# Ten per-head scalings of a delta-rule front moved from VectorE to ScalarE, head by head

## The reference

```
x  = hidden + attention(layernorm(hidden));  out = x + experts(layernorm(x))

# attention, per head h
q, k, v = silu(conv(xn @ W)) each;  q, k = q/|q|, k/|k|;  beta = sigmoid(xn @ Wb)
for each token t:
    u = beta * (v - k . S);   S = S + k u^T;   o = q . S
out = (o normalized per head) @ Wo
```

## Time and profile before

| what | value |
|---|---|
| median of 3 executions | 1375.21 us (1373.84 to 1380.05) |
| the profiled execution | 1386.45 us, its span 1384.7 us |
| mean granted TensorE clock over the span | 0.968 of full speed |
| share of the span busy | PE 96%, DVE 63%, ACT 27%, POOL 24% |
| PE, DVE, ACT busy in 200 to 250 us | 47.41, 37.13, 25.32 of 50 us |
| PE, DVE, ACT busy in 300 to 350 us | 45.91, 43.10, 25.93 of 50 us |

### The profile page before, as it was taken

The page is one execution under the profiler, slowest core; times in us unless marked ns, Lnnn a source line. Parts: engine busy times, 40 slices in busy tenths (PEclk is TensorE's granted clock), DMA queues, the critical chain, the costliest instruction groups (busy, mean ns, idle before and its releaser), DMA issues.

```text
span 1384.7 us, 27271 instructions
## 1 busy us (share of the span) xinstructions
PE 1329.5 (96%) x8490; PEld 841.0 (61%) x8491; DVE 867.6 (63%) x2418; ACT 371.2 (27%) x794; POOL 338.6 (24%) x396
## 2 busy tenths in 40 slices
PE   8979999999999999999999999999999999999996
PEld 7857777887777556544444455555555555555553
DVE  4896687559556512725311177777777777777774
ACT  4635554545443223212000011111111111111111
POOL 1201223223121221311565112221222122222222
PEclk9989999999998799999999999999999999999998
DMA  4205643734474794397545746656766665664430
GB/s 154 61 6 112 100 91 77 133 93 95 89 122 114 137 236 107 70 164 244 189 179 206 244 78 129 136 128 132 176 149 134 126 133 128 131 133 76 70 52 5
DMA packets 208513, 171.05 MB, mean 124 GB/s; under 512 B 71472, under 2 KB 160560, under 8 KB 208432
## 3 DMA queue, kind: packets, MB, share of 16 engines
q1 hardware_dynamic: 135056, 114.16, 33.7%
q0 software_dynamic: 16496, 34.23, 12.7%
q10 hardware_dynamic: 56880, 21.54, 7.7%
HBM read 91.06 MB, written 82.73 MB: 126 GB/s over the span
## 4 chain that ended last, share of the span: by engine, by line
PE 52%; DVE 2%; issue 0%; POOLq 0%; DVEq 0%; ACT 0%
PE pD L2059 15%; PE pG L2039 13%; PE pU L2048 13%; PE pG L2003 3%; PE pU L2003 3%; PE pD L2022 3%; DVE ups L1950 1%; PE pU L1997 0%; PE pD L2017 0%; POOLq L1777 0%; DVE w L1676 0%; DVE w L1677 0%; DVE route_keep L1675 0%; DVE q L1695 0%; DVE qf L1688 0%
## 5 line engine op out<-in xcount | busy, mean ns | idle before, releaser
L1950 DVE STREAM_TRANSPOSE ups<-a 32x96 f32<-32x96 f32 (+1 forms) x1264 | 330.1, 261 | 42.9
L1847 POOL DMA_INDIRECT out<-y,ix x79 | 123.0, 1556 | 481.3 <-ACT y L1903 332.7
L2059 PE MATMUL pD<-w,ups 128*128 (+1 forms) x474 | 218.3, 596 | 3.6 <-DVE ups L1950 3.6
L2039 PE MATMUL pG<-w,xsT 128*128 x632 | 199.9, 458 | 0.0
L2048 PE MATMUL pU<-w,xsT 128*128 x632 | 199.9, 459 | 0.0
L2039 PEld LDWEIGHTS pG<-w,xsT 128*128 128x128 f32 x632 | 119.5, 189 | 88.4 <-issue 37.6
L902 PE MATMUL pProj<-front_region 128*128 128x256 f32 x624 | 159.5, 400 | 2.2 <-ACT front_region L682 1.4
L2048 PEld LDWEIGHTS pU<-w,xsT 128*128 128x128 f32 x632 | 120.1, 190 | 66.9
L2059 PEld LDWEIGHTS pD<-w,ups 128*128 128x128 f32 (+1 forms) x474 | 90.7, 192 | 97.8 <-issue 81.5
L1243 DVE SCALAR_TENSOR_TENSOR front_region<-front_region,cw 128x256 f32<-128x256 f32 x288 | 132.4, 501 | 15.5 <-ACT front_region L698 12.1
L902 PEld LDWEIGHTS pProj<-front_region 128*128 128x128 f32 x624 | 115.8, 195 | 21.8 <-ACT front_region L698 2.9
(11 more groups left out here) (236 smaller groups left out, 1623.2 us busy)
## 6 DMA issues: line engine op xcount, KB each, us to landing
w<-in_up_T SPq DMA_DIRECT2D x16, 1408.0 KB, 6.7
slot_rows<-zeros SPq DMA_DIRECT2D x79, 266.0 KB
xs<-slot_rows ACTq DMA_DIRECT2D x316, 64.0 KB
w<-in_down_T SPq DMA_DIRECT2D x16, 512.0 KB, 8.7
front_region<-in_L_attn_hidden_states SPq DMA_DIRECT2D x16, 256.0 KB, 3.1
x2r<-in_L_attn_hidden_states SPq DMA_DIRECT2D x16, 256.0 KB, 5.5
partial_sums<-x2r SPq DMA_DIRECT2D x16, 256.0 KB, 3.6
x_normed<-x2n SPq DMA_DIRECT2D x16, 256.0 KB, 2.6
```

What stands on the lines that cost most here:

```text
L1847: pool.indirect_dma_start(out=flat, out_offset=bass.IndirectOffsetOnAxis(ap=ix[1 - par][:, 0:1], axis=0), in_=y[1 - par][:, :], in_offset= ...
L1950: dve.transpose(aT[par][B * to:B * to + B, 0:n, rows], a[rows, 0:len(IC) * P].rearrange("p (c n) -> p c n", c=len(IC))[:, 0:n, B * to:B * ...
L2039: mm = pe.matmul(pG[0][:, 0:I], xsT[par][:, k, :], w[:, bass.ds(slot, 1), 2 * I * k:2 * I * k + I], start=(k == 0), stop=(k == DC - 1))
L2059: mm = pe.matmul(pYq[:, :], aT[1 - par][0:m, c, :], down[0:m, :, UPW + D * c:UPW + D * (c + 1)], start=(c == 0), stop=(c == 2))
```

## The change

Six tiles' values (6, 7, 10, 11, 14, 15) and four tiles' Gram blocks (8, 9, 12, 13) are scaled on ScalarE. There a factor is one number for each partition, so that each head is an instruction of its own: eight `activation` of 128x64 with a factor from `sqk` or `ng` in place of one `tensor_tensor` of 128x512 on VectorE. They stand in these places: values of the even tile in slot 5 of the even unit (2, 6, 10), behind `raw_copy`; values of the odd tile in slot 0 of the odd unit (3, 7, 11), behind `x_copy`; Gram blocks in slots 3 and 5 of units 3 and 7, behind `oT_copy` in slot 3 and ahead of `w_copy` in slot 5. The semaphores and what waits for them are as before.

```diff
--- before.py
+++ after.py
@@ -60,6 +60,7 @@
 NUP = DC + 2 * DC * (UNITS - 1)
 NMM = NUP + TPG * UNITS
 EARLY_MM = NMM + DC + 2 * DC
+V_ON_ACT, GRAM_ON_ACT = (6, 7, 10, 11, 14, 15), (8, 9, 12, 13)
 FILL_AT, FILL = (11, 3), 2
 XG_AT = SHARED_W
 SA_AT = XG_AT + 2 * DC * GN
@@ -681,6 +682,26 @@
                 least(act, s_bp, p - 1)
                 act.activation(xnT[p % 2][:, :, tok(t)], quads(pT0[:, 0, :]), ACT.Copy).then_inc(s_xnT, 1)
 
+            def scale_v(t):
+                act.wait_ge(s_vtp, t + 1)
+                act.wait_ge(s_coef, t // 2 + 1)
+                least(act, s_R, 2 * (t - VH_RING) + 2)
+                for h in range(H):
+                    ins = act.activation(vh[t % VH_RING][:, cols(h)], pT0[:, 0, cols(h)], ACT.Copy,
+                                         scale=sqk[t // 2 % 2][:, H * (t % 2) + h:H * (t % 2) + h + 1])
+                ins.then_inc(s_vh, 1)
+
+            def scale_blocks(t):
+                act.wait_ge(s_G, t + 1)
+                act.wait_ge(s_ng, t // 2 + 1)
+                least(act, s_Xp, t - NP_RING + 1)
+                for f in range(2):
+                    for n in range(HH):
+                        h = H * (t % 2) + 2 * n + f
+                        ins = act.activation(NP[t % NP_RING][:, cols(HH * f + n)], pG[:, f, cols(n)], ACT.Copy,
+                                             scale=ng[t // 2 % 4][:, h:h + 1])
+                ins.then_inc(s_N, 1)
+
             def tanh(p):
                 act.wait_ge(s_bp, p + 1)
                 least(act, s_hb, p)
@@ -814,6 +835,10 @@
                         x_copy(u)
                     if even and s == (0 if pk else 1) and pair_ok(pk) and pk != 1:
                         tanh(pk)
+                    if even and s == 5 and 2 * old in V_ON_ACT and old > 1:
+                        scale_v(2 * old)
+                    if not even and s == 0 and u + 4 in V_ON_ACT and u + 4 > 3:
+                        scale_v(u + 4)
                     if opening(u, s) in (1, 2):
                         make_xn(opening(u, s) + 1)
                     if opening(u, s) in (2, 3):
@@ -850,6 +875,8 @@
                         x2T_copy(u - 2)
                     if s == 3 and tile_ok(u - 1):
                         oT_copy(u - 1)
+                    if not even and s in (3, 5) and u + 5 + s // 4 in GRAM_ON_ACT:
+                        scale_blocks(u + 5 + s // 4)
                     if s == 5 and tile_ok(u + 1):
                         w_copy(u + 1)
                     for n in range(EARLY_UNITS):
@@ -1272,6 +1299,8 @@
                 dve.tensor_reduce(ssq[:, cols(t % 2, H)], by_head(sq[t % 2][:, :]), AX.X, ALU.add).then_inc(s_qss, 1)
 
             def make_v(t):
+                if t in V_ON_ACT:
+                    return
                 dve.wait_ge(s_vtp, t + 1)
                 dve.wait_ge(s_coef, t // 2 + 1)
                 least(dve, s_R, 2 * (t - VH_RING) + 2)
@@ -1280,6 +1309,8 @@
                    .then_inc(s_vh, 1)
 
             def scale_gram(t):
+                if t in GRAM_ON_ACT:
+                    return
                 dve.wait_ge(s_G, t + 1)
                 dve.wait_ge(s_ng, t // 2 + 1)
                 least(dve, s_Xp, t - NP_RING + 1)
```

## The result

With the change the kernel takes 1384.14 us (median of 20 executions, 1379.47 to 1397.47), the kernel before 1377.89 us (median of 20). The ratio is 1.0067, 95% interval 1.0048 to 1.0086: some 9 us slower. The two medians lie 6.3 us apart and the two means 9.8; where this text says 9 us, it goes by the ratio.

The account below looks back on a forecast made before the run. TensorE, busy 96% of the span, was taken to bound the kernel with its pauses. Pauses of 5.5 + 5.2 + 1.3 - 3.9 = +8.1 us and 4.8 of clock made +13, from 1375.21 to 1388 us, range 1378 to 1400.

Parts of the forecast that it names:

- Eight scalings: On ScalarE, eight per-head scalings of one tile or block take 1.71 us, where VectorE took 0.69.
- Pause A: Second value transpose, units 2, 6, 10: TensorE waits 1.83 us for scaled values, three times, 5.5 us.
- Pause B: Key transpose, units 3 and 7: TensorE waits 2.62 us behind the odd tile's scaling, 5.2 us in all.
- Pause D: Merge, units 4 and 8: `merge_x` waits 0.67 us for `Wt` copies behind block scaling, 1.3 us in all.
- What is taken away: Units 3 and 7: `Rs` pauses shrink from 5.99 to 2.8 us and 0.69 of `vh` goes: 3.9 us gained.
- Pauses together: Net TensorE pauses: 5.5 + 5.2 + 1.3 - 3.9 = +8.1 us.
- The clock: Half-clock stretches behind pauses, one each in units 2/3, 6/7 and 10: between +2.4 and +7.2, taken as +4.8 us.
- second rival: Each new pause in units 2/3, 6/7 and 10 starts its own slow stretch: +23.5 us, 1399; chance 0.18.
- Sum: Whole kernel: 8.1 us of pauses and 4.8 of clock, +13 us, median 1388.
- c = 3.1: Upper bound, in us, for eight scalings on ScalarE; the forecast then gives +9.8 us, said to reach past the range.
- first rival, whole relief: Units 3 and 7 lose `Rs` pauses and slow stretches, 11.5 us: no change (1376), chance 0.17, or faster, 0.05.

Follow-up runs that it names:

- padded change: The change, with VectorE keeping a 128x512 multiplication in each of the ten places, against the kernel before: ratio 1.0075.
- second profile of the change: The changed kernel run once more, unaltered, for another profile, against the kernel before: ratio 1.0066.
- early version: The same ten scalings on ScalarE, but placed where it stood idle, against the kernel before: ratio 0.9938.
- padded and unpadded early versions: Scalings placed where ScalarE is idle, with or without a 128x512 VectorE multiplication kept in each of ten places: ratios 1.0013 and 0.9938 against before.

## Why the prediction was right

The forecast of a slower kernel held; 1388 us lies 4 us above the median of 1384.14, and the time is inside the range of 1378 to 1400. The forecast stood on a median of three executions, 1375.21; on the 1377.89 of twenty the same +13 would have been 1391. By its steps:

- **Eight scalings.** 1.71 us predicted, 1.75 measured. Each took 0.335 us (values) or 0.352 (blocks), not 0.31, at 0.20 us from start to start. The estimate of 2.0 by the Trainium skill ("ScalarE: Activation LUTs", section "What ACT_TABLE_LOAD costs") was 0.25 too high.
- **Pause A.** 1.83 predicted; 1.86, 1.86 and 1.83 measured.
- **Pause B.** 2.62 predicted; 2.74 twice.
- **Pause D.** 0.67 predicted; in the change it didn't appear. It shows when the blocks move alone (0.51) or when the load is out of the way (0.31). The term was real but stood in the shadow of another that I missed: the wait of `merge_w` for `TT`'s load, 1.17 and 1.96 us. I had looked at who waits for the Gram store and not at what stands behind it on SyncE's queue, where the inverse's store and load feed TensorE. Before, the inverse's store was issued at 225.74 and `merge_w` ran at 234.96, 9.2 us later, without a wait; in the change it waited and ran 7.0 us after the store (233.89 and 240.93). So, by this count, the slow stretch behind the long `Rs` pause (`out_proj` 5.97 us, now 3.70) had covered that chain.
- **What is taken away.** I left 1.4 us of each `Rs` pause; 0.74 was left, so the term was 1.3 us too small. VectorE took 229.32 + 0.69 - 219.25 = 10.8 us from `logits` to the end of the residual, not 11.6. The difference is one multiplication, below. The padded change shows that the mechanism that I gave (VectorE gains no more than it trails `gate` by, since `logits` waits behind pause B) held.
- **Pauses together.** +8.1 predicted. Measured by name, in units 2 to 8 it is 13.8 - 6.7 = +7.1. In 10 and 11 come 1.83 for `vh`, and 0.94 in place of 1.38 us for `TT`'s scaling: +8.5 in all. That this meets the forecast is in part luck: the load's 3.1 us, which I had at nothing, stand against 1.3 us of pause D that didn't come, 1.3 us more taken off the `Rs` pauses, and 0.4 in unit 11.
- **The clock.** +4.8 predicted. The mean granted clock fell from 0.9743 to 0.9716 and 0.9701; over some 1380 us that is 3.7 and 5.8 us. Filling the pauses kept the clock at 1.00 behind them and gave back some 4 us, so these pauses cause slow stretches. The profile of the change has the three that I counted: the clock held through pause A in units 2 and 6 and fell behind B in 3 and 7, and in unit 10 it fell behind A. But which pause is followed moves. In the second profile of the change `hop_r` (L1016) and the projection behind pause A of unit 6 were slow, and those behind pause B of unit 7 as well:

```profile
333.83 1.09 PE L1016 MATMUL pC<-S,kq 64*64 64x64 f32 x16
334.85 3.19 PE L929 MATMUL pProj<-front_region 128*128 128x256 f32 x8
...
343.48 3.78 PE L929 MATMUL pProj<-front_region 128*128 128x256 f32 x8
```

So the second rival, in which each pause has a stretch of its own, came in this place of this execution and not as a whole. One stretch for each pair was a guess: the first profile has three stretches behind these five pauses, the second four.
- **Sum.** +13 predicted, +9.2 measured (0.67% of 1377.89), while the measured parts add to 12 to 14. TensorE's idle time in two long windows (length and PE busy are the first two numbers) of before:

```profile
195.00:450.00 255.00, 244.45 (x3135) 0.94 0.49 102
450.00:640.00 190.00, 176.76 (x1541) 0.91 0.72 153
```

and of the change:

```profile
195.00:450.00 255.00, 238.25 (x3011) 0.95 0.43 96
450.00:640.00 190.00, 179.30 (x1666) 0.95 0.70 163
```

To 450 us idle time rises by 6.2, near the named +7.1; behind 450, where the shared experts are woven in, it falls by 2.5, though there the named pauses rise. In the second profile of the change it fell by 0.8. So up to a few us are given back at the front's end, where other waits rule. How much of that is the kernel's and how much chance between executions stays open.

One bound of the range was misread: with c = 3.1 the forecast's +9.8 us lead to 1398 us, not past the 1400, so the range did hold it.

The first rival, whole relief, needed the pauses covered; as the change stands they aren't. The early version comes nearest to it: no pause for ScalarE's scalings is left, though 5.0 us of `Rs` pauses are.

## What to carry to other kernels

Work that is moved to an idle engine costs nothing only at the place where that engine is idle and its input is already there; at the next convenient line it waits for whatever stands ahead, and the tensor engine with it. Ask of each moved result when its consumer wants it, what must run ahead of it in the new list, and what stands behind it on every queue, DMA queues included. A pause on TensorE can cost more than its length, and relief for a late engine pays once only: pauses elsewhere may already have given it.

## What the hardware showed that I had not expected

Of VectorE's and GpSimd's larger multiplications one waits while the other runs, and the profile shows the wait as a longer instruction. In the kernel before VectorE multiplied 128x768 in 1.80 us:

```profile
213.65 1.80 DVE L1381 TENSOR_TENSOR prod_b<-route_keep,zc 128x768 f32<-128x768 f32 x1
```

while GpSimd's multiplication of 128x512, begun 1.14 us earlier, together with VectorE's of 128x1024 (212.51, 1.22 us), took 2.13:

```profile
212.51 2.13 POOL L625 TENSOR_TENSOR osb<-osb,ro 128x512 f32<-128x512 f32 x1
```

In the change they fell apart, GpSimd's to 216.47, when VectorE waited for `logits`:

```profile
216.47 1.04 POOL L626 TENSOR_TENSOR osb<-osb,ro 128x512 f32<-128x512 f32 x1
```

and VectorE alone (the row at 222.32, between `logits` and the residual):

```profile
219.25 0.17 DVE L1352 COPY lg<-pT 128x16 f32<-128x16 f32 x1 [4.62 <-PE pT L1077]
...
222.32 0.95 DVE L1412 TENSOR_TENSOR prod_b<-route_keep,zc 128x768 f32<-128x768 f32 x1
...
229.32 0.69 DVE L1332 TENSOR_TENSOR Rs<-pC,vh 64x512 f32<-64x512 f32 x1
```

0.95 in place of 1.80 us, and 1.04 in place of 2.13. The ends fit turns: GpSimd's ended at 214.64, about a microsecond after VectorE's 128x1024, and VectorE's 128x768 at 215.45, 0.81 after that. The Trainium skill ("SBUF — State Buffer", section "Who interferes with whom") names a port pair that VectorE and GpSimd share under an exclusive lock; these rows agree with it. It accounts for the 11.6 us that became 10.8 in the reckoning of the `Rs` pauses: shifting one engine's work by some us changed the length of another's instruction. The same 128x768 multiplication is 1.80 us again in both padded and unpadded early versions, where the two overlap. In the unpadded one GpSimd's, begun at 213.46, when VectorE's 128x1024 was nearly through, took 1.10 us: there only VectorE's was long.
